# First LayerNorm's subtraction and scaling moved from VectorE to GpSimd

## The reference

```
x  = x + proj(softmax attention of 8 heads of 32 channels over 1024 tokens, on GroupNorm(x))
t  = tokens of x                                  # 1024 x 256
n  = LN1(t)                                       # (t - mean) / sqrt(var + 1e-5), over 256 channels
t  = t + linear attention(n) + depthwise conv of width 3 along the tokens (n)
r  = LN2(t)
t  = t + inverse Haar(MLP(upsampled low band of r), other bands of r)
```

## Time and profile before

| | us |
|---|---|
| median of 3 runs | 1364.84 (1364.63 to 1365.78) |
| profiled execution, its own time | 1364.11 |
| its span, first to last instruction | 1362.3 |
| PE busy | 1235.3 (91%) |
| DVE busy | 995.1 (73%) |
| ACT busy | 879.5 (65%) |
| POOL busy | 467.4 (34%) |

### The profile page before, as it was taken

How to read it: one execution, slowest core, us unless ns; L and a number is a source line. 1 busy time by engine, 2 the same in 40 slices (tenths; PEclk the granted TensorE clock), 3 DMA queues, 4 the chain that set the end, 5 groups by cost and what they waited for, 6 DMA issues and landing times.

```text
span 1362.3 us, 22187 instructions
## 1 busy us (share of the span) xinstructions
PE 1235.3 (91%) x7972; PEld 644.5 (47%) x7972; DVE 995.1 (73%) x1609; ACT 879.5 (65%) x1457; POOL 467.4 (34%) x621
## 2 busy tenths in 40 slices
PE   6888899899998999899998999989998999979796
PEld 5544444544445454445444444454544444444373
DVE  3666687857889487866888578884879678884663
ACT  1666667675776668676775767766685767757422
POOL 2001017520285015630185203840166301850351
PEclk9998999999999999999999999999999999999897
DMA  8242415123442236223351234422262234300210
GB/s 275 58 108 45 106 40 134 34 63 101 110 112 47 52 109 139 48 63 93 92 116 27 66 117 101 105 57 58 88 140 48 62 93 110 80 15 0 80 33 31
DMA packets 51180, 110.84 MB, mean 81 GB/s; under 512 B 15456, under 2 KB 15840, under 8 KB 50816
## 3 DMA queue, kind: packets, MB, share of 16 engines
q1 hardware_dynamic: 48400, 100.39, 30.3%
q0 software_dynamic: 2480, 8.78, 2.3%
q10 hardware_dynamic: 192, 0.26, 0.1%
HBM read 21.81 MB, written 8.39 MB: 22 GB/s over the span
## 4 chain that ended last, share of the span: by engine, by line
PE 54%; DVE 29%; ACT 7%; issue 4%; POOL 2%; DMA 2%; SPq 1%; DVEq 0%; ACTq 0%; POOLq 0%
DVE negmax L1053 15%; PE ps_s L653 13%; PE ps_o L668 7%; PE work L741 6%; ACT probs L914 5%; PE work L680 4%; PE work L800 4%; PE work L727 4%; PE work L692 3%; DVE tok L1129 3%; DVE ln_st L1118 3%; PE work L805 3%; PE work L781 2%; DVE lo L1098 1%; PE work L715 1%
## 5 line engine op out<-in xcount | busy, mean ns | idle before, releaser
L914 ACT ACTIVATE probs<-ps_s,negmax 128x1024 f32<-128x1024 f32 x512 | 571.0, 1115 | 328.0 <-DVE negmax L1053 323.3
L1053 DVE TENSOR_REDUCE negmax<-ps_s 128x1 f32<-128x1024 f32 x512 | 618.8, 1216 | 220.0 <-PE ps_s L653 218.2
L653 PE MATMUL ps_s<-q_st,k_st 128*128 128x512 f32 x1024 | 407.8, 482 | 54.7 <-ACT probs L914 42.7
L653 PEld LDWEIGHTS ps_s<-q_st,k_st 128*128 128x128 f32 x1024 | 165.1, 192 | 294.4 <-ACT probs L914 163.3
L1330 POOL TENSOR_TENSOR v_scaled<-v_tok,rsums 128x128 f32<-128x128 f32 x128 | 56.0, 438 | 580.3 <-DVE rsums L1059 580.3
L668 PE MATMUL ps_o<-probs,v_scaled 128*32 128x512 f32 x2048 | 249.9, 606 | 1.3 <-POOL v_scaled L1330 1.3
L680 PE MATMUL work<-xg,w_qkv 128*128 128x512 f32 x256 | 120.7, 597 | 2.7 <-ACT xg L927 2.7
L741 PE MATMUL work<-ln_ch,w_qk 128*128 128x512 f32 x240 | 115.0, 601 | 3.6 <-DVE k_ch L1236 3.6
L668 PEld LDWEIGHTS ps_o<-probs,v_scaled 128*32 128x32 f32 x2048 | 53.9, 110 | 129.9 <-issue 117.7
L1389 POOL TENSOR_TENSOR x<-x,csum 128x1024 f32<-128x1024 f32 x45 | 107.5, 2389 | 2.5
L914 ACT ACTIVATION_READ_ACCUMULATOR probs<-ps_s,negmax 128x1 f32 x512 | 99.6, 195 | 0.0
(11 more groups left out here) (157 smaller groups left out, 1448.5 us busy)
## 6 DMA issues: line engine op xcount, KB each, us to landing
q_st<-hi SPq DMA_DIRECT2D x128, 128.0 KB, 2.4
q_st<-lo SPq DMA_DIRECT2D x120, 128.0 KB, 2.4
k_st<-t SPq DMA_DIRECT2D x224, 64.0 KB, 2.0
k_st<-hi SPq DMA_DIRECT2D x128, 64.0 KB, 2.8
k_st<-lo SPq DMA_DIRECT2D x128, 64.0 KB, 3.2
x<-in_x SPq DMA_DIRECT2D x8, 1024.0 KB, 6.1
out_x<-ln_ch SPq DMA_DIRECT2D x16, 512.0 KB, 2.8
xg<-in_x POOLq DMA_DIRECT2D x7, 1024.0 KB, 8.6
```

Of the source, the lines that this page charges most:

```text
L653: mm = pe.matmul(ps_s[s % 2][:, half * HALF:half * HALF + HALF], k_st[:, h, j * P:j * P + P], q_st[g][:, h, half * HALF:half * HALF + HALF ...
L914: act.activation(probs[:, j % 2, h, :], ps_s[s % 2][:, :], ACT.Exp, bias=negmax[:, s % 4:s % 4 + 1], accum_out=sums[:, j % 2, h:h + 1]).th ...
L1053: dve.tensor_reduce(negmax[:, s % 4:s % 4 + 1], ps_s[s % 2][:, :], AX_X, ALU.max, negate=True)\
```

## The change

The function `ln_normalise` moves out of VectorE's program and gets the engine as its first argument. The step "norm1" leaves the tables `DVE_STEADY` and `DVE_LAST` and enters `POOL_STEADY` and `POOL_LAST` at the slots of "rsqrt1": (10, 11, 13, 14) and (9, 9, 14, 15). In the table it stands behind "rsqrt1", so in a shared slot all roots of the slot come first. The epilogue's tables keep it on VectorE, and "norm2" stays on VectorE everywhere (its branch in GpSimd's program is not reached by any table).

```diff
 DVE_STEADY = {
-    "pv0": (47, 63), "norm1": (11, 14, 16, 16), "norm2": (42, 45, 46, 47), "pk1": (21, 21), "proj": (5, 7, 8, 9),
+    "pv0": (47, 63), "norm2": (42, 45, 46, 47), "pk1": (21, 21), "proj": (5, 7, 8, 9),
...
 POOL_STEADY = {
...
-    "affine": (40,), "rsqrt1": (10, 11, 13, 14), "lepe": (16, 21, 22, 22, 23, 23, 24, 25, 25, 25, 25, 26),
+    "affine": (40,), "rsqrt1": (10, 11, 13, 14), "norm1": (10, 11, 13, 14), "lepe": (16, 21, 22, 22, 23, 23, 24, 25, 25, 25, 25, 26),
...
 DVE_LAST = {
-    "norm1": (11, 14, 16, 16), "invert": (0, 4, 8, 12, 16, 20, 24, 28, 32, 36, 41, 45, 47, 51, 57, 61),
+    "invert": (0, 4, 8, 12, 16, 20, 24, 28, 32, 36, 41, 45, 47, 51, 57, 61),
...
 POOL_LAST = {
-    "scale": (3, 9, 9, 12, 16, 20, 24, 28, 32, 36, 42, 46, 50, 53, 56, 61), "rsqrt1": (9, 9, 14, 15),
+    "scale": (3, 9, 9, 12, 16, 20, 24, 28, 32, 36, 42, 46, 50, 53, 56, 61), "rsqrt1": (9, 9, 14, 15), "norm1": (9, 9, 14, 15),
...
+        def ln_normalise(eng, b, n, src, rsqrt, done):
+            eng.wait_ge(rsqrt, 4 * b + n + 1)
+            for t in range(2):
+                nm = eng.tensor_scalar(tok[:, 2 * n + t, :], src(t), ln_mv[:, n, t, 0:1],
+                                       ln_rs[:, n, t:t + 1], ALU.subtract, ALU.mult)
+            nm.then_inc(done, 1)
...
                 elif name == "norm1":
-                    ln_normalise(b, n, x1_tokens(n), ln1_rsqrt, ln1_done)
+                    ln_normalise(dve, b, n, x1_tokens(n), ln1_rsqrt, ln1_done)
                 elif name == "norm2":
-                    ln_normalise(b, n, t2_tokens(n), ln2_rsqrt, ln2_done)
+                    ln_normalise(dve, b, n, t2_tokens(n), ln2_rsqrt, ln2_done)
...
+                elif name == "norm1":
+                    ln_normalise(pool, b, n, x1_tokens(n), ln1_rsqrt, ln1_done)
```

More of the change, by code:

```diff
@@ L514, in turn_q, with x1_tokens, t2_tokens @@
                 eng.tensor_tensor(q_ch[:, g, :], q_ch[:, g, :], q_half[g], ALU.add).then_inc(qrot_done[g], 1)
+        def ln_normalise(eng, b, n, src, rsqrt, done):
[4 more added lines that the diff above has]
+            nm.then_inc(done, 1)
+        def x1_tokens(n):
+            return lambda t: tok[:, 2 * n + t, :]
+        def t2_tokens(n):
+            return lambda t: t2[:, 2 * n + t, :]
         def add_norm(eng, b, n):
@@ L1124, in ln_statistics @@
                 ag.then_inc(step, 1)
[L1126 to L1137, removed]
             def four_heads(ap):
@@ L1418, in step @@
                     mean_keys(b)
+                elif name == "norm1":
+                    ln_normalise(pool, b, n, x1_tokens(n), ln1_rsqrt, ln1_done)
+                elif name == "norm2":
+                    ln_normalise(pool, b, n, t2_tokens(n), ln2_rsqrt, ln2_done)
                 elif name == "lepe":
```

## The result

The changed kernel takes 1383.86 us (median of four runs, 1381.03 to 1386.53), the kernel before 1365.31 on the same occasion: ratio 1.0135, 95% interval 1.0115 to 1.0155, 18.5 us slower. Forecast were 1357.1, and the range ended at 1361.0. The prediction was wrong, in sign too.

What follows compares the result with a forecast made beforehand. VectorE's chain was taken to bound the changed stage, TensorE full behind it. Seven images by 1.10 us gave 7.7 us off, 1356.4 for the profiled execution, 1357.1 by the median; range 1351.5 to 1361.0.

Steps and rivals of the forecast that it cites:

- What bounds the kernel: In the changed stage VectorE's chain sets the pace, TensorE nearly full; behind it TensorE is full.
- steps 1 to 4: Slot 14's scores to the last root's first operation, put at 359.69; may be off by 0.3 us per image.
- step 1: Slot 14: VectorE, some 0.7 us ahead, waits for TensorE's scores; its maximum starts at 355.57, before 355.69.
- step 3: ScalarE's exponential and copy of the last token tile hold the last statistics until 358.58, against 359.25 before.
- The new price of a pair: GpSimd's normalisation at 256 columns: 0.45 us per operation, 0.86 for two in a row.
- step 5: Power, pair and hand-over before the third tile of transposes to channels: it starts at 361.72, 1.10 us earlier.
- rival D: Last pair takes 2.4 us, through width-independent time or VectorE holding GpSimd: 3.1 us slower, 1367.9; chance 0.03.
- The bounds: GpSimd's normalisation operation takes 0.30 to 0.61 us: gain 1.4 to 0.78 us per image, 1355.0 to 1359.4.
- What hides the rest: First three pairs sit in GpSimd's waits; in the last middle image two run together; both costed at nothing.
- A: Third tile of transposes starts when TensorE is ready, 1.71 us earlier: 12.0 in all, 1352.8; chance 0.21.
- B: The lead is given back at a later stage before the image ends: 1362 to 1365 us; chance 0.06.
- C: Pair at the speed of GpSimd's scaling, 1.60 us: gain 2.5, 1362.3; chance 0.06, including up to the forecast.

Runs made afterwards that it cites:

- e4: The changed kernel with ten unused 128x128 matmuls in TensorE's wait before the third tile of transposes to channels: ratio 1.0004, on another chip 1.0017.
- e1: The kernel before, with GpSimd `tensor_scalar` probes behind its last instruction; only durations read: at 256 columns subtract, multiply 1.22 us, multiply, add 0.55.
- e7: The kernel before with normalisation tiles 0 to 2 on GpSimd as add, multiply (negated mean), tile 3 on VectorE: 1361.17 us (0.9957), again 1357.10 (0.9950).

## Why the prediction was wrong

*What bounds the kernel, and steps 1 to 4:* right. Two rows of VectorE after the change (the maximum of slot 14, then the last statistics):

```profile
358.77 1.23 DVE L1066 TENSOR_REDUCE negmax<-ps_s 128x1 f32<-128x1024 f32 x1 [0.29 <-PE ps_s L666]
...
361.81 0.75 DVE L1131 BATCH_NORM_STATS2 ln_st<-tok 128x6 f32<-128x256 f32 x2
```

VectorE does wait for TensorE before the maximum of slot 14, as step 1 said. The statistics of the last tile start at 12.11 in their stage; step 3 gave 358.58 in a stage begun at 346.48, which is 12.10. In the kernel with multiply, add the root's first operation starts at 13.22, forecast 13.21.

*The new price of a pair, and step 5:* this is the step that failed. I took a price from the row of L1386, same instruction and operand kinds, and scaled it by columns. I did not look at the operations: L1386 multiplies and adds, the normalisation subtracts and multiplies. The term was 0.86 us for the pair and measured 2.43. At this price a second cost enters that no part of the prediction had, rival D included: the clock that falls at the longer wait, some 1.6 us in each of six images (e4). Even for the fast form 0.45 was low: the fixed part is 0.34, not the 0.20 of a 2-column operation, and the pair measured 1.09. With that number in step 5 the forecast tile comes out at 15.47, and 15.52 was measured.

*The bounds:* the upper one, 0.61 from L1395, is a two-tensor add, a form that happens to be fast, and I let it exclude everything above. It bounded another instruction, not this one. No row before showed GpSimd doing a `tensor_scalar` with subtract. The range should have been open to that side. Rival D held 0.03 for a pair of 2.4 us, which is what came. But it named two causes, a time that doesn't depend on the width and a collision, and neither was at work (e1), so its price was right by luck. I gave it so little because the row of L1395 seemed to leave only the collision. VectorE's way into SBUF played no part that the traces show: 56 operations within 18 ns. The Trainium skill, "GPSIMD Engine Reference", Engine selection, puts elementwise work with one input about even with VectorE; measured are 1.22 us to 0.41 for this form, so the rule doesn't hold for it, and 0.55 to 0.41 for the fast one.

*What hides the rest:* right only at the forecast price, and wrong for the last body, where I cost two pairs in a row at nothing and the tile came 1.7 us late. Four pairs of 2.43 us with their roots filled GpSimd from 352.41 to 366.75. The last root started at 13.53 in the stage, 0.31 us after its statistics allowed.

*Rival D's price:* 0.44 us per image for a pair of 2.4. Measured are 0.86 for the tile: the 0.31 of queueing and 0.11 of small terms were missing from it. And it held no term for the clock, 1.59 us in the median image, more than the delay itself. The sign would have been right and the size, 3.1 us, a sixth of what came. The trace before could have told. At another place, 22 to 24 us behind the group means, TensorE waits 0.82 to 1.10 us for ScalarE (L996) ahead of the MLP's first matmuls, and the granted clock falls there in four middle images of six. Two windows of the kernel before at that place:

```profile
285.99:289.99 4.00, 4.00 (x7) 1.86 (x8) 0.00 (x0) 3.24 (x5) 0.00 (x0) 0.57 0.84 185
761.26:765.26 4.00, 3.40 (x9) 1.16 (x7) 1.22 (x1) 3.18 (x5) 0.00 (x0) 1.00 0.45 96
```

At the group means themselves, behind a wait of 1.46 to 1.63 us, it falls in two of the six. From uT to the next stage's start it is 87.1 and 87.2 us in the images with no fall, 88.1 and 88.3 with the one at the MLP, and 89.7 and 89.6 with both. So a fall of the clock near a wait costs 1.0 to 1.6 us here. At these places it comes in some images only; behind the 3.0 us it came in six of seven, in both executions.

*Rivals A to C:* A's mechanism, TensorE ready earlier, is seen in e7 as a remaining wait of 0.96. B did not occur: in the kernel with multiply, add 5.3 us are gained up to the tile over the seven images (109.1 against 114.4), and the distance behind it is not longer (368.0 against 370.9, and 2.6 of that is the fourth image, 52.63 against 55.23). C's price, 1.60 for the pair, was above the forecast and still below 2.43.

## What to carry to other kernels

Price a moved instruction from a row with the same engine, instruction, operand kinds and the same operations; if there is none, measure that form alone before moving it, or keep the range open on that side (here other operations made the same instruction 2.2 times as long at 256 columns and 3.2 times at 1024). Move to the slower engine the pieces that have room, and keep the last link before the bounding engine where it is fastest: in the slow form three tiles of four gained 0.4 to 0.7%, and the fourth turned that into a loss of 1.35%. And when a change makes TensorE wait longer, add what a lower clock behind the wait costs to the wait itself.

## What the runs showed of the hardware

- GpSimd, `tensor_scalar`, float32, two per-partition operands, 128 partitions: multiply, add; add, multiply; and multiply, multiply take 0.55 us at 256 columns; subtract, multiply; multiply, subtract; and add, add take 1.22. Multiply, add grows by 0.83 ns a column, subtract, multiply by 3.33.
- One operation alone takes 0.92 us at 256 columns, longer than a fast pair; subtract, multiply with immediates 1.07.
- TensorE's granted clock stood at 0.50 for some 3 us at or behind a wait of 3.0 us in six images of seven (in two executions), and stayed at 1.00 behind waits of 0.96 to 1.40 us in the same place. Ten small matmuls in the wait, which left about 0.76 us of it idle, kept it at 1.00 in all seven. At another place, behind waits of 0.82 to 1.10 us, it fell in four images of six, so the length of the last wait alone doesn't decide it.
- One such fall costs 1.0 to 1.6 us of this kernel's time.
